# Top-32 attention and a routed FFN on one core: selection work moved to GpSimd, marking to ScalarE, weight splitting to VectorE

## The reference

```python
q, k, v = LN(x) @ Wq.T + bq, ctx @ Wk.T + bk, ctx @ Wv.T + bv      # 16 heads of 16 channels
scores = q @ k.T / 4; scores[mask == 0] = -1e9
vals, idx = top_k(scores, 32)                                     # 32 of 1024 keys for each query
attn = (softmax(vals) @ v[idx]) @ Wo.T + bo
x = x + tanh(g_xattn) * attn
# 8 experts (256 -> 1024 -> 256), the two best for each token, capacity 640 for each choice
x = x + tanh(g_ffn) * moe(LN(x)),  expert(t) = (silu(t @ Wg.T) * (t @ Wu.T)) @ Wd.T
```

## Time and profile before

| | us |
|---|---|
| median of three runs | 3287.62 (3280.4 to 3288.7) |
| the profiled execution | 3283.47 |
| its span | 3281.7 |

### The profile page before, as it was taken

How to read it: one execution, slowest core, us unless ns; L and a number is a source line. 1 busy time by engine, 2 the same in 40 slices (tenths; PEclk the granted TensorE clock), 3 DMA queues, 4 the chain that set the end, 5 groups by cost and what they waited for, 6 DMA issues and landing times. The chain is left out here.

```text
span 3281.7 us, 64952 instructions
## 1 busy us (share of the span) xinstructions
PE 2536.3 (77%) x17723; PEld 1599.8 (49%) x17724; DVE 2788.9 (85%) x20206; ACT 1460.3 (44%) x1991; POOL 1915.2 (58%) x1393
## 2 busy tenths in 40 slices
PE   7837787887787778787788778753645999999998
PEld 4512333333333333333333333322544999999998
DVE  6739999999999999999999999956554777777775
ACT  2205666666666666666666666631111222222222
POOL 1017888888888888888888888840163233232231
PEclk9968999999999999999999999985767999999999
DMA  6961211212112112112121121101232222222221
GB/s 189 260 185 31 64 37 31 61 37 45 48 37 64 29 37 64 29 41 59 29 56 45 29 64 37 29 12 41 89 115 93 61 64 62 52 57 62 50 40 20
DMA packets 131053, 201.23 MB, mean 61 GB/s; under 512 B 22816, under 2 KB 97824, under 8 KB 127616
## 3 DMA queue, kind: packets, MB, share of 16 engines
q1 hardware_dynamic: 112768, 167.56, 18.9%
q0 software_dynamic: 17920, 29.52, 4.3%
HBM read 129.60 MB, written 69.50 MB: 61 GB/s over the span
## 5 line engine op out<-in xcount | busy, mean ns | idle before, releaser
L568 DVE MAX8 a_cand<-a_sc 128x8 f32<-128x43 f32 (+1 forms) x12288 | 1646.0, 193 | 50.3 <-ACT a_sc L509 50.2
L670 POOL TENSOR_SCALAR a_side<-a_sc,a_top 128x1024 bf16<-128x1024 f32 x512 | 1455.9, 2844 | 333.1 <-DVE a_top L602 329.4
L509 ACT COPY a_sc<-a_ps_s 128x1024 f32<-128x1024 f32 x512 | 518.3, 1012 | 781.2 <-POOL a_side L670 720.4
L520 ACT ACTIVATE a_pT<-a_ps_e 128x1024 f32<-128x1024 f32 x512 | 526.3, 1028 | 15.2 <-PE a_ps_e L440 11.4
L419 PE MATMUL a_ps_s<-a_ks,a_qs 96*128 96x512 bf16 x1024 | 319.6, 395 | 246.1 <-ACT a_sc L509 192.5
L433 PE MATMUL a_ps_e<-a_qs,a_ks 99*128 99x512 bf16 x1024 | 317.0, 392 | 179.5 <-ACT a_pT L520 178.6
L1402 POOL DMA_INDIRECT out<-e_y,e_xin x80 | 124.0, 1550 | 558.9 <-ACT e_y L1535 516.4
L472 PE MATMUL a_ps_o<-a_pT,a_vs 128*32 128x512 f32 x2048 | 429.0, 693 | 1.1 <-ACT a_pT L520 1.1
L1467 PE MATMUL e_ps_gu<-e_xh,e_wl 128*128 128x256 f32 x1280 | 368.2, 288 | 54.6 <-DVE e_h L1587 49.5
L1468 PE MATMUL e_ps_gu<-e_xl,e_wh 128*128 128x256 f32 x1280 | 365.1, 285 | 0.0
L1469 PE MATMUL e_ps_gu<-e_xh,e_wh 128*128 128x256 f32 x1280 | 364.8, 285 | 0.0
(11 more groups left out here) (201 smaller groups left out, 4163.2 us busy)
## 6 DMA issues: line engine op xcount, KB each, us to landing
scr_v<-p_vp SPq DMA_DIRECT2D x32, 512.0 KB, 6.0
a_vs<-scr_v SPq DMA_DIRECT2D x32, 512.0 KB, 5.7
a_mask<-in_mask SPq DMA_DIRECT2D x32, 512.0 KB, 6.6
scr_k<-p_kp SPq DMA_DIRECT2D x96, 128.0 KB, 2.4
a_ks<-scr_k SPq DMA_DIRECT2D x32, 384.0 KB, 4.6
a_qs<-scr_q SPq DMA_DIRECT2D x192, 64.0 KB, 5.2
scr_disp<-a_blank SPq DMA_DIRECT2D x16, 650.0 KB, 8.2
e_xin<-scr_disp SPq DMA_DIRECT2D x40, 260.0 KB, 2.8
```

The lines of the kernel that those rows point to most:

```text
L509: nc.scalar.copy(sc[:, T % 4, :], ps_s[:]).then_inc(copied, 1)
L520: nc.scalar.activation(pT[:, 2 * n:2 * n + 2, :].rearrange("p k q -> p (k q)"), ps_e[:], ACT.Exp).then_inc(expd, 1)
L568: ins = nc.vector.max(c[:, 8 + n:8 + n + 7 * CH + 1:CH], sc[:, T % 4, pl.cut[n]:pl.cut[n + 1]])
L670: nc.gpsimd.tensor_scalar(side[:, T % SIDES, :], sc[:, T % 4, :], top[:, T // TILES % 2, T % TILES, pl.TOPK - 1:pl.TOPK], None, ALU.is_lt) ...
```

## The change

1. **attend, selection.** Two of the three culls leave VectorE. The second eight are removed by GpSimd in `sink_two`, and the third eight in `sink`: each one `tensor_scalar` (compare with the last value of the eight, times -3e38) and one `tensor_tensor` add that waits for it, over 48 and over 80 candidates. The last two rounds run one and two steps later.
2. **attend, marking.** GpSimd marks only tiles with qt = 0 (`OWN = 1`). For qt = 1, 2 and 3 ScalarE marks with `Sign(next_under - score)`, which is +1 below the 32nd value and -1 at or above it; `next_under`, a value just below the 32nd, is made by two small GpSimd instructions. On TensorE a product of ones and `floor` now opens the accumulation for three of the four query blocks and adds -2^100 there; the marks follow, the scores come last and close it. `sc` has 7 buffers, marking and everything behind it starts two steps later.
3. **repair, test.** `lows` is compared with two numbers: 128 x (1024 - 32) for `slice(0, half)` of the index qt and 128 x (1024 - 64) for `slice(half, QT)`, with `half = QT // 2`.
4. **repair, v.** The load of v is issued from ScalarE's queue, behind exp, and ScalarE waits for `v_free`.
5. **experts.** The low parts are made on VectorE, each matrix in four pieces of 512 columns, one piece behind each of the feature blocks 1 to 4 of a chunk (and all at once for the first expert). GpSimd keeps only the scattered adds.

```diff
-    FIRST = 7
+    FIRST = 9
+    SCORES = 7
+    OWN = 1
+    REST = QT - OWN
-    END = NT + 12
+    END = NT + 15
+        def sided_by(T):
+            h, n = divmod(T, QT)
+            return (sided[0], h * OWN + n + 1) if n < OWN else (sided[1], h * REST + n - OWN + 1)
@@ mark (TensorE)
-                    nc.tensor.matmul(ps_e[:, i * S:(i + 1) * S], ks[:, u, j, keys], qs[:, u, j, :], start=True, stop=False)
...
+                    nc.tensor.matmul(ps_e[:, i * S + OWN * P:(i + 1) * S], onesb[:], floor[:], start=True, stop=False)
                     for qt in range(QT):
-                        mm = nc.tensor.matmul(..., big[:], start=False, stop=qt == QT - 1)
+                        nc.tensor.matmul(..., big[:], start=False, stop=False)
+                    mm = nc.tensor.matmul(ps_e[:, i * S:(i + 1) * S], ks[:, u, j, keys], qs[:, u, j, :],
+                                          start=False, stop=True)
@@ ScalarE, in every step after copy(s + 1)
+            def to_sides(T):
+                act.wait_ge(under_set, T // QT * REST + T % QT - OWN + 1)
+                if T >= SIDES:
+                    act.wait_ge(marked, PAIRS * ((T - SIDES) // QT + 1))
+                nc.scalar.activation(side[:, T % SIDES, :], sc[:, T % SCORES, :], ACT.Sign, bias=next_under[:, T % 8:T % 8 + 1],
+                                     scale=-1.0).then_inc(sided[1], 1)
+                if 0 <= s - 5 < NT and (s - 5) % QT >= OWN:
+                    to_sides(s - 5)
@@ VectorE, in every step
-                        elif p % 2 == 0:
-                            cull(T, p // 2 - 1)
-                        else:
-                            round_of(T, (p - 1) // 2)
+                        elif p == 2:
+                            cull(T)
+                    if p == 5 and 0 <= s - 2 < NT:
+                        round_of(s - 2, 2)
+                    if p == 6 and 0 <= s - 3 < NT:
+                        round_of(s - 3, 3)
@@ GpSimd
+            def step_under(T):
+                n = T // QT * REST + T % QT - OWN + 1
+                pool.wait_ge(topped[1], T + 1)
+                last = top[:, T // TILES % 2, T % TILES, pl.TOPK - 1:pl.TOPK]
+                one = slice(T % 8, T % 8 + 1)
+                nc.gpsimd.tensor_scalar(gap[:, one], last, 1.0 + 2.0 ** -23, -2.0 ** -124, ALU.mult, ALU.add
+                                        ).then_inc(gap_set, 1)
+                pool.wait_ge(gap_set, n)
+                nc.gpsimd.tensor_scalar(next_under[:, one], last, 1.0 - 2.0 ** -24, gap[:, one], ALU.mult, ALU.min
+                                        ).then_inc(under_set, 1)
+            def sink_two(T):
+                src, g = cand[:, T % 4, 8:8 + 2 * CH], gone_two[:, T % 2, :]
+                pool.wait_ge(picked, 2 * T + 2)
+                nc.gpsimd.tensor_scalar(g, src, top[:, T // TILES % 2, T % TILES, 15:16], TAKEN, ALU.is_ge, ALU.mult
+                                        ).then_inc(found_two, 1)
+                pool.wait_ge(found_two, T + 1)
+                nc.gpsimd.tensor_tensor(src, src, g, ALU.add).then_inc(sunk_two, 1)
+            def sink(T): (the same with 80 candidates and top 23:24, into `left`)
+            for s in range(NT + 2):
+                if s < NT:
+                    sink_two(s)
+                if 0 <= s - 1 < NT:
+                    sink(s - 1)
+                T = s - 2
+                if T >= 0 and T % QT < OWN:
+                    to_sides(T)
+                elif T >= 0:
+                    step_under(T)
@@ repair
-                take(sp, v_free)
-                sp.dma_start(v[:], scr["v"]...[I, :, :, j, :]).then_inc(in_v, 16)
@@ repair, ScalarE, behind exp of the same tile
+                take(act, v_free)
+                act.dma_start(v[:], scr["v"]...[I, :, :, j, :]).then_inc(in_v, 16)
@@ repair, VectorE
-            link(V.tensor_scalar(bad[:].rearrange("p (i n) -> p n i", n=TILES), flat[:], float(P * (S2 - pl.TOPK)), None,
-                                 ALU.not_equal))
+            of_tile = bad[:].rearrange("p (i j t) -> p j t i", j=HG, t=QT)
+            sums = flat[:].rearrange("p (j t) i -> p j t i", t=QT)
+            half = QT // 2
+            for h, right in ((slice(0, half), P * (S2 - pl.TOPK)), (slice(half, QT), P * (S2 - 2 * pl.TOPK))):
+                ins = V.tensor_scalar(of_tile[:, :, h], sums[:, :, h], float(right), None, ALU.not_equal)
+            link(ins)
@@ experts, GpSimd: cut_weight is gone, add_rows(C) in turn; VectorE:
+            def cut_weight(e, u, n, i):
+                part = slice(i * PART, (i + 1) * PART)
+                if i == 0:
+                    dve.wait_ge(w_high, 3 * e + n + 1)
+                nc.vector.tensor_tensor(wl[:, u, n, part], raw[:, (u + n) % 2, part], wh[:, u, n, part].bitcast(F32),
+                                        ALU.subtract).then_inc(w_cut, 1)
...
+                        if turns and 0 < f <= PIECES:
+                            cut_weight(e + 1, 1 - u, c - NCH + 3, f - 1)
```

More of the change, by code:

```diff
@@ L329, in attend @@
         above = sb("a_above", [P, 2, TILES, 2])
+        gone = sb("a_gone", [P, 2, 8 + NA])
+        gone_two = sb("a_gone_two", [P, 2, 2 * CH])
+        left = sb("a_left", [P, 2, 8 + NA])
+        gap = sb("a_gap", [P, 8])
+        next_under = sb("a_next_under", [P, 8])
         rest = sb("a_rest", [P, 2, QT])
@@ L359, in attend @@
         culled = sem("a_culled")
-        topped = sem("a_topped")
+        topped = [sem(f"a_topped{n}") for n in (2, 3)]
+        found = sem("a_found")
+        sunk = sem("a_sunk")
+        found_two = sem("a_found_two")
+        sunk_two = sem("a_sunk_two")
+        gap_set = sem("a_gap_set")
+        under_set = sem("a_under_set")
         odd_part = sem("a_odd_part")
@@ L429, in mark @@
                     pe.wait_ge(expd, PAIRS * H + n)
+                if n == 0:
+                    pe.wait_ge(sided[0], OWN * (H + 1))
+                    pe.wait_ge(sided[1], REST * (H + 1))
                 for i in range(2):
@@ L432, in mark @@
                     keys = slice(k * P, (k + 1) * P)
-                    nc.tensor.matmul(ps_e[:, i * S:(i + 1) * S], ks[:, u, j, keys], qs[:, u, j, :], start=True, stop=False)
[L434 to L438, removed]
+                    nc.tensor.matmul(ps_e[:, i * S + OWN * P:(i + 1) * S], onesb[:], floor[:], start=True, stop=False)
                     for qt in range(QT):
-                        mm = nc.tensor.matmul(ps_e[:, i * S + qt * P:i * S + (qt + 1) * P],
-                                              side[:, (QT * H + qt) % SIDES, keys], big[:], start=False, stop=qt == QT - 1)
+                        nc.tensor.matmul(ps_e[:, i * S + qt * P:i * S + (qt + 1) * P], side[:, (QT * H + qt) % SIDES, keys],
+                                         big[:], start=False, stop=False)
+                    mm = nc.tensor.matmul(ps_e[:, i * S:(i + 1) * S], ks[:, u, j, keys], qs[:, u, j, :],
+                                          start=False, stop=True)
                 mm.then_inc(marked, 1)
@@ L488, in _ @@
                     mark(H, n)
-                if 0 <= s - 4 < NT:
-                    count(s - 4)
+                if 0 <= s - 6 < NT:
+                    count(s - 6)
                 H, n = head_at(s, FIRST + 2)
@@ L701, in cut_peaks @@
                 nc.gpsimd.tensor_tensor(p3, r, p2, ALU.subtract).then_inc(peaked, 1)
-            for s in range(2, NT + 2):
-                to_sides(s - 2)
-                H, n = head_at(s, 4)
+            for s in range(NT + 2):
[8 more added lines that the diff above has]
+                    step_under(T)
+                H, n = head_at(s, 3)
                 if H is not None and n == 0:
                     cut_peaks(H)
-                if (s - 2) % TILES == TILES - 1:
-                    find_odd((s - 2) // TILES)
+                if T >= 0 and T % TILES == TILES - 1:
+                    find_odd(T // TILES)
 def repair(nc, pl, io, scr, keep):
@@ L1339, in experts @@
     NCH = 2 * CAP // R
-    DX, XB, LATE = pl.DX, 4, 2
-    assert CAP % P == 0
+    DX, XB = pl.DX, 4
+    PIECES = 4
+    PART = KD * F // PIECES
+    assert CAP % P == 0 and FB >= PIECES + 2
     with ExitStack() as ctx:
@@ L1569, in expert @@
                     cut_x(C, s)
-                    if c >= NCH - 3 and not last:
+                    turns = c >= NCH - 3 and not last
+                    if turns:
                         high_weight(e + 1, 1 - u, c - NCH + 3, start and u == 0)
@@ L1596, in _ @@
                 high_weight(0, 0, n, True)
+                for i in range(PIECES):
+                    cut_weight(0, 0, n, i)
             expert(0, 0, True)
```

90 lines of the change are left out of this document (44 added, 46 removed).

## The result

The changed kernel takes 5097.55 us (median of four runs, 5094.99 to 5099.4) against 3288.16 before: 1.551 times as long, 95% interval 1.548 to 1.554. The forecast was 5090.

The account below looks back on a forecast made before the run. VectorE was taken to bound attend, TensorE experts, and a chain of waits repair. From 3283.5 us, -160 (attend), +2025 (repair) and -60 (experts) gave 5089, stated as 5090; range 4960 to 5290.

Parts of the forecast that it names:

- The list: Repair's test: all 128 tiles with qt = 1 are listed through a wrong constant, about 132 instead of 5.
- A listed tile: Repair: with v out of the queue, 15.75 us a tile instead of 21.2; bounds 14.9 and 16.5.
- the second tile's 0.81 us gap: Repair before: the second tile, its loads behind no wait, followed after 0.81 us; taken as the new steady gap.
- Loads late: Rival, repair: q and k loads still wait, 128 more tiles at 21.2 us, 5790 us in all; chance 0.04.
- The list loop: Repair: eight tiles a turn, 17 turns for one, 2.6 us each; 16 more are 41 us.
- Attend: Attend, selection: two culls leave VectorE, 0.31 us a tile, -160 us; bounds a gain of 189 and a loss of 60.
- The upper prices: Attend: GpSimd compare-and-multiply at 0.5 and 0.65 us; four tiles then take 13.7 us and more with waits.
- all three fit: Attend: GpSimd (11.8), ScalarE (12.1) and TensorE (13.3) fit in VectorE's 13.5 us for four tiles, two barely.
- the rival that I gave 0.07: Attend: GpSimd or TensorE becomes the bound at 3.87 us a tile, 5310 us in all; chance 0.07.
- Experts: Experts: without GpSimd's cuts the collisions with VectorE's subtractions end, -60 us; bounds -20 and -62.
- the short list: Rival, repair: the constants fit after all or the index was misread, five tiles listed, 3042 us; chance 0.06.
- All three quarters: Rival, repair: no ScalarE sum is 128 x 960, so 384 + 1 tiles are listed, 9160 us; chance 0.04.

Follow-up runs that it names:

- e5: Kernel before, with only its repair test comparing the tiles with qt = 1 with the wrong number (128 x 960): 6038.6 us.
- e1: Changed kernel with half = 1 in repair's test, so all three quarters that ScalarE marks are compared with 128 x 960: 3078.92 us, 0.937 of before.
- e7: Changed kernel with half = 3 in repair's test, so qt = 1 and qt = 2 are both compared with the wrong number: 7148.27 us.
- e6: Kernel before, with the wrong test number for qt = 1 and v's load on ScalarE's queue behind exp: 5337.62 us.
- e2: Changed kernel with OWN = 2 and nothing else, so GpSimd marks qt = 0 and 1: 3314.06 us, 1.009 of before.
- e12: e1 without the GpSimd instruction for gap, next_under made from the 32nd value alone: 9167.73 us, 2.791 of before.
- e10: Kernel before with GpSimd's weight subtraction of 128 x 2048 cut into four of 128 x 512, still on GpSimd: 3318.68 us, 1.009 of before.

## Why the prediction was right

- **The list** (+128 tiles) was read from the code alone, by comparing what ScalarE writes with what the test expects. 132 were forecast, 133 came, since none of the 5 of before has qt = 1 (e5); e1 and e7 move the list by the quarter and nothing else does.
- **A listed tile**: 15.75 forecast, 15.84 measured. The step from the second tile's 0.81 us gap was right; the steady gap is 0.92. Two readings beside it were not. The scores come 12.2 us behind the first q load and not some 8, by TensorE's own order and not by the loads, and what hides this has 0.7 us to spare. And in the earlier trace rows the scores are ready at 2246.24 + 1.03 = 2247.27, 1.5 us before the copy at 2248.82; the mask stands on the same queue behind k, is issued at 2244.90 and lands in a median of 3.4 us, so it comes last by this estimate (2248.3), and the idle time is the queue's all the same. Loads late (5790) falls by the 15.84, and e6 against e5 shows that the queue is what counts. The list loop: 2.6 forecast, 2.32 measured.
- **Attend**: -160 forecast, -168 measured, and partly by luck. VectorE's share was right (3.38 at best, 3.42 measured). GpSimd was put at 11.8 of 13.5 us for four tiles; with its gaps it takes 13.6 of 13.7. Two terms were small: a `tensor_scalar` of two operations costs 0.47 and 0.56, between the interpolated 0.34 and 0.42 and the upper 0.50 and 0.65, and gaps were counted only inside each sink and each `step_under`, at 0.07. A `step_under` takes 0.61 and not 0.47 (0.19 + 0.11 + 0.315). The adds were less than forecast (0.285 and 0.353). The upper prices add up to 13.3 and not to 13.7 (four tiles of 0.91 + 1.14, with 1.4 and 3.73). TensorE was put at 13.3 and takes 884.8 / 293 x 4 = 12.1, so it was not barely in time but had 1.6 us to spare; its clock was 1.00 where the row that the forecast started from had 0.95, and what share of the difference this is was not tested. ScalarE was right, 12.1 against 12.3. For GpSimd "all three fit" was true by 5 us in 1000; e2 shows the other side of that edge, 3.91 us a tile, which is the price of the rival that I gave 0.07.
- **Experts**: -60 forecast, -67 measured. The start gave 4.1 (5 forecast) and the idle time 49.6 (54.6 before, 5.0 after; the forecast took all 54.6 for the collisions'). The term that I left out is the clock: in `experts` before, six windows of 20 us in which there are collisions stand at 0.91 to 0.92, one of them here,
```profile
2740.00:2760.00 20.00, 17.95 (x140) 17.74 (x138) 15.48 (x30) 3.98 (x10) 7.68 (x3) 0.92 0.26 62
```
  and after, from 4380 us on, all stand at 1.00 but the first and the last. Not every collision shows this: there are 21, and the windows of the others stand at 0.99 or 1.00. What tells them apart is not known. A loss of 0.09 in 20 us is 1.8 us, 11 us in six; that is most of the 13.6 that are left (67.3 - 4.1 - 49.6). The 84 of VectorE's 96 pieces of 0.69 us that lie in the loop cost TensorE nothing, as forecast: its groups show no wait for them.
- **The sum**: attend came 8 us below its term, experts 7 below, repair 26 above (one tile more, 0.09 us more on each of 132, the list 4 less). They cancel to 11, so that 5090 lies within 8 us of 5097.55 is in part luck.
- **The rivals**: the short list was priced 3042. With 8 tiles in place of 5 it is 3079, and by the 15.84 would have been 3032 with 5. All three quarters was priced 9160; e12 came there by another road, at 9168.

## What to carry to other kernels

A value that one stage writes and another tests is part of the same edit: when three places know a split (who marks, what a mark is worth, which total is expected), derive all of them from one constant, here `OWN`. A safety net that recomputes what fails hides such a slip from the output and shows it only in the time, so count how often it runs. When an engine takes over work, add the gaps between its dependent instructions to their durations before you call it free.

## What was not expected of the hardware

- Four GpSimd subtractions without a wait between them, 5.54 us together, hold off a VectorE subtraction with two operands in SBUF no less than one of 5.15 us does (6.18 us against 5.78): a shorter instruction is no remedy, a pause between them might be. The pause wasn't tried.
- A wait of TensorE of some 2.4 us in a stage that is else full can cost more than itself: with 20 waits of 2.4 us on average the granted clock of the stage before is 0.98 (2560 to 3281 us), with 20 of 2.7 us in e10 it is 0.94 (2560 to 3300), without them 1.00. No wait is longer than 2.6 us before and 3.0 in e10. That the 0.3 us more in each wait is the reason for e10's lower clock was not tested by itself.
- The 384 marks by Sign among the exps take 1.16 us each (1.06 for the Sign of the earlier trace rows), and the trace after has the same single table load on the exp line.
